# Casting x straight into its region of the activation buffer, and normalizing it there in place, in an eight-core attention and gated-MLP layer

## The reference

```python
xn = layernorm(x)                          # mean and variance over 1024 features
q, k, v = split(xn @ Wqkv + bqkv)          # 3 x 1024
q, k = q / norm(q), k / norm(k)
kv = sum over all 4096 tokens of k * v     # one row of 1024 for each batch
attn = (q * kv) @ Wout + bout
h = silu(xn @ w1.T * s1) * (xn @ w2.T * s2)      # 4096 wide
h = gelu(h @ h1.T * t1); h = gelu(h @ h2.T * t2)
out = x + attn + h @ w3.T * s3
```

## Time and profile before

| what | us |
|---|---|
| the runs shown, both | 3056.84 and 3350.54, median 3203.69 |
| the profiled execution | 3057.52 |
| its span on the slowest core (core 5) | 3055.7 |
| spans of the other cores | 3011.9 to 3048.4 |
| TensorE (PE) busy on core 5 | 2877.9 (94% of the span) |
| DVE, ACT busy | 378.7 (12%), 464.8 (15%) |
| loads of x, all through SP | 96 of 512 KB |
| loads of weights, through POOL | 416 of 512 KB landed |

### The profile page before, as it was taken

How to read it: one execution, slowest core, us unless ns; L and a number is a source line. 1 busy time by engine, 2 the same in 40 slices (tenths; PEclk the granted TensorE clock), 3 DMA queues, 4 the chain that set the end, 5 groups by cost and what they waited for, 6 DMA issues and landing times.

```text
span 3055.7 us, 30723 instructions; the slowest of 8 cores (3011.9 to 3055.7 us)
## 1 busy us (share of the span) xinstructions
PE 2877.9 (94%) x13056; PEld 1282.4 (42%) x13056; DVE 378.7 (12%) x440; ACT 464.8 (15%) x463; POOL 219.9 (7%) x420
## 2 busy tenths in 40 slices
PE   3887999899999999999987899999999999999998
PEld 0332444344444444444433344444444444444433
DVE  3255211451000000000012221100000000000011
ACT  1453211441000000000020031110000000000100
POOL 0000000110000000000000000000000000000000
PEclk8988999999999999999988999999999999999999
DMA  6555344875444444444446544444444444444453
GB/s 161 133 134 128 73 77 75 173 130 91 76 76 76 76 76 76 76 76 77 76 102 133 125 81 79 74 77 77 77 77 78 77 76 77 76 76 76 76 111 89
DMA packets 76598, 278.93 MB, mean 91 GB/s; under 512 B 8752, under 2 KB 8880, under 8 KB 76464
## 3 DMA queue, kind: packets, MB, share of 16 engines
q0 software_dynamic: 59904, 218.13, 43.1%
q1 hardware_dynamic: 16560, 58.85, 6.2%
HBM read 486.66 MB, written 8.39 MB: 162 GB/s over the span
## 4 chain that ended last, share of the span: by engine, by line
PE 83%; DMA 5%; DVE 2%; ACT 1%; issue 0%; SPq 0%; DVEq 0%; ACTq 0%
PE PD L198 23%; PE PC L198 23%; PE PB L198 19%; PE PA L198 18%; DMA xs<-x_fm 4%; DMA out_fm<-os 1%; DVE os L703 1%; DVE os L697 0%; ACT os L669 0%; DVE tmp_f L259 0%; DVE xb L210 0%; ACT Ab L628 0%; DVE Ab L500 0%; DVE Gb L261 0%; DVE tmp_f L237 0%
## 5 line engine op out<-in xcount | busy, mean ns | idle before, releaser
L198 PE MATMUL PC<-Gb,wr 128*128 128x512 bf16 x2080 | 476.3, 381 | 26.5 <-DVE Gb L261 26.5
L198 PE MATMUL PD<-Gb,wr 128*128 128x512 bf16 x2080 | 477.3, 382 | 0.0
L198 PE MATMUL PB<-Gb,wr 128*128 128x512 bf16 x1728 | 392.8, 381 | 4.2 <-DVE rstd_b L242 4.2
L198 PE MATMUL PD<-Ab,wr 128*128 128x512 bf16 x1536 | 357.7, 387 | 40.4 <-ACT os L669 40.4
L198 PE MATMUL PC<-Ab,wr 128*128 128x512 bf16 x1536 | 348.9, 380 | 2.1 <-ACT os L669 2.1
L198 PE MATMUL PA<-Gb,wr 128*128 128x512 bf16 x1536 | 347.2, 379 | 0.0
L198 PEld LDWEIGHTS PC<-Gb,wr 128*128 128x128 bf16 x2080 | 203.4, 98 | 277.9 <-issue 36.0
L198 PEld LDWEIGHTS PD<-Gb,wr 128*128 128x128 bf16 x2080 | 205.1, 99 | 250.0 <-issue 8.5
L198 PEld LDWEIGHTS PB<-Gb,wr 128*128 128x128 bf16 x1728 | 169.4, 98 | 210.5 <-issue 8.1
L191 POOL DMA_DIRECT2D wr<-h_t x256 | 135.1, 528 | 1616.6 <-PE PB L198 798.4
L198 PEld LDWEIGHTS PD<-Ab,wr 128*128 128x128 bf16 x1536 | 152.4, 100 | 231.0 <-issue 57.4
(11 more groups left out here) (87 smaller groups left out, 1002.8 us busy)
## 6 DMA issues: line engine op xcount, KB each, us to landing
wr<-h_t POOLq DMA_DIRECT2D x256, 512.0 KB, 5.2
xs<-x_fm SPq DMA_DIRECT2D x96, 512.0 KB, 5.0
wr<-w_t POOLq DMA_DIRECT2D x96, 512.0 KB, 5.7
wr<-wqkv_t POOLq DMA_DIRECT2D x56, 512.0 KB, 5.8
out_fm<-os SPq DMA_DIRECT2D x16, 512.0 KB, 3.3
wr<-wout_t POOLq DMA_DIRECT2D x8, 512.0 KB, 5.8
cst<-consts SPq DMA_DIRECT2D x1, 64.0 KB, 1.9
ones_sb<-ones_bf SPq DMA_DIRECT2D x1, 32.0 KB, 2.7
```

The costliest lines, as they stand in the source:

```text
L198: e.matmul(p[:, h * 512:(h + 1) * 512], l, r, start=a, stop=b),
```

## The change

In plan_stats a new argument via_region (true unless given) casts x into its own region of Gb, not into xb. Squares and sums read it from there. The cast waits until the region is free. In the second pass the product reads the bf16 chunk from Gb, and no second load of x is made; the subtraction overwrites the chunk in place, after the chunk's own square and sum have been read (chunk_toks). The call for group 5, made while h2's input has just been read from Gb, keeps the old way (via_region=False). Group 3 moves from region 0 to region 1, since its cast now happens while the gate still reads group 4 in region 0. So xn is now computed from x rounded to bf16. Of the 96 loads of x, 32 go: the second ones of groups 0, 1, 2 and 3.

```diff
-REGION = {0: 0, 1: 1, 2: 2, 3: 0, 4: 0, 5: 2}
+REGION = {0: 0, 1: 1, 2: 2, 3: 1, 4: 0, 5: 2}
...
-                jb, bslot, fb = xb_ring.next()
-                tb = S.op("vector", lambda e, o=bslot, i=xslot: e.tensor_copy(o[:, :], i[:, :]),
-                          waits=[tx, fb], inc="s_dv")
+                if via_region:
+                    tb = S.op("vector", lambda e, g_=g, c_=c, i=xslot: e.tensor_copy(
+                        xn_sl(g_, c_), i[:, :]),
+                        waits=[tx, war[REGION[g]]], inc="s_dv")
+                    sq_src = xn_sl(g, c)
+                else:
+                    (as before)
...
-                tq = S.op("scalar", lambda e, o=qslot, i=bslot: e.activation(o[:, :], i[:, :], AF.Square),
+                tq = S.op("scalar", lambda e, o=qslot, i=sq_src: e.activation(o[:, :], i, AF.Square),
...
-                    tok_s = mm(psS, hh, ones_sb[:, :], bslot[:, hh * 512:(hh + 1) * 512],
+                    rhs = xn_sl(g, c, hh) if via_region else bslot[:, hh * 512:(hh + 1) * 512]
+                    tok_s = mm(psS, hh, ones_sb[:, :], rhs,
...
-                xb_ring.set_free(jb, [tok_s, tq])
+                if via_region:
+                    chunk_toks[c] = [tok_s, tq]
+                else:
+                    xb_ring.set_free(jb, [tok_s, tq])
...
             def emit_xn(c):
-                jx, xslot, tx = dma_x(c, t0)
-                ta = S.op("vector", lambda e, i=xslot: e.tensor_mul(tmp_f[:, :], i[:, :], rstd_b[:, :]),
-                          waits=[tx, t5], inc="s_dv")
+                if via_region:
+                    ta = S.op("vector", lambda e, g_=g, c_=c: e.tensor_mul(
+                        tmp_f[:, :], xn_sl(g_, c_), rstd_b[:, :]),
+                        waits=[t5], inc="s_dv")
+                    tb2 = S.op("vector", lambda e, g_=g, c_=c: e.tensor_tensor(
+                        xn_sl(g_, c_), tmp_f[:, :], u_b[:, :], ALU.subtract),
+                        waits=[ta, t6, chunk_toks[c]], inc="s_dv")
+                else:
+                    (as before)
...
-                    emit_xn = plan_stats(g + 1, "PA", "PB", defer_xn=True)
+                    emit_xn = plan_stats(g + 1, "PA", "PB", defer_xn=True,
+                                         via_region=False)
```

More of the change, by code:

```diff
@@ L199, in mm, with plan_stats @@
                         waits=waits, inc=inc)
-        def plan_stats(g, psS="PA", psQ="PB", defer_xn=False):
+        def plan_stats(g, psS="PA", psQ="PB", defer_xn=False, via_region=True):
             t0 = T0MAP[g]
@@ L204, in plan_stats @@
             last_q = [None]
+            chunk_toks = {}
             for c in range(DC):
@@ L208, in plan_stats @@
                 jx, xslot, tx = dma_x(c, t0)
-                jb, bslot, fb = xb_ring.next()
-                tb = S.op("vector", lambda e, o=bslot, i=xslot: e.tensor_copy(o[:, :], i[:, :]),
-                          waits=[tx, fb], inc="s_dv")
+                if via_region:
[4 more added lines that the diff above has]
+                else:
+                    jb, bslot, fb = xb_ring.next()
+                    tb = S.op("vector", lambda e, o=bslot, i=xslot: e.tensor_copy(o[:, :], i[:, :]),
+                              waits=[tx, fb], inc="s_dv")
+                    sq_src = bslot[:, :]
                 xs_ring.set_free(jx, tb)
                 jq, qslot, fq = sq_ring.next()
-                tq = S.op("scalar", lambda e, o=qslot, i=bslot: e.activation(o[:, :], i[:, :], AF.Square),
+                tq = S.op("scalar", lambda e, o=qslot, i=sq_src: e.activation(o[:, :], i, AF.Square),
                           waits=[tb, fq], inc="s_ac")
@@ L257, in emit_xn @@
             def emit_xn(c):
-                jx, xslot, tx = dma_x(c, t0)
-                ta = S.op("vector", lambda e, i=xslot: e.tensor_mul(tmp_f[:, :], i[:, :], rstd_b[:, :]),
-                          waits=[tx, t5], inc="s_dv")
[L261 to L264, removed]
+                if via_region:
[6 more added lines that the diff above has]
+                else:
+                    jx, xslot, tx = dma_x(c, t0)
+                    ta = S.op("vector", lambda e, i=xslot: e.tensor_mul(tmp_f[:, :], i[:, :], rstd_b[:, :]),
+                              waits=[tx, t5], inc="s_dv")
+                    tb2 = S.op("vector", lambda e, g_=g, c_=c: e.tensor_tensor(
+                        xn_sl(g_, c_), tmp_f[:, :], u_b[:, :], ALU.subtract),
+                        waits=[ta, t6, war[REGION[g]]], inc="s_dv")
+                    xs_ring.set_free(jx, ta)
                 xn_toks.append(tb2)
```

## The result

| | before | changed |
|---|---|---|
| median of all runs, us | 3060.45 (10 runs) | 3025.17 (11 runs) |
| mean of the runs that the ratio compares, us | 3056.5 (7 runs) | 3020.4 (8 runs) |
| profiled execution, slowest core's span | 3055.7 (core 5) | 3013.3 (core 6) |
| mean span of the eight cores, profiled execution | 3032.3 | 2998.3 |
| loads of x | 96 | 64 |

The ratio of changed to before is 0.9882, 95% interval 0.9856 to 0.9908: a gain of 36 us, 1.2%; the interval leaves out 1, and the gain lies within the 2% that stood for "same". The forecast was 3027. Executions in which the cores of one die or of both took longer at a lower granted clock are left out of the ratio; one of them is why the two runs first shown lay 294 us apart.

A forecast was written before the change was run, and what follows sets the result against it. TensorE fills 94% of the slowest core's 3055.7 us, so only its waits can give time back. Terms 6 + 7.5 + 6.4 + 10.9 = 30.8 us, from 3057.5, gave 3027; own range 3015 to 3036, chance 0.70.

The forecast's parts named there:

- k-projection 1: First block, with xn(1): without reloads TensorE's waits for normalized chunks and the lower clock after them go; 7.5 us saved.
- segment 1: Second block: xn(3) ends earlier without reloads, so this segment runs as long as segment 2; 10.9 us saved.
- stats(2): Group 2's statistics, first block: casts start earlier after the kv sums, 12.4 us left of 18.9; 6.4 us saved.
- xn(0): Group 0's normalization at the start: product from Gb taken at 1.23 us, no wait for x before; 0 us saved.
- stats(1): Group 1's statistics, first block: casts follow their loads without waiting for xb slots; 6 us saved.
- stats(3): Group 3's statistics: loads issued only in the second block, wait on region 1 already over; 0 us saved.
- A: Rival: block 1's gain goes to the loads, x still late for stats(1) and stats(2); 18.4 us left, 3039; chance 0.12.
- B: Rival: nothing reaches the end, the slowest core waits elsewhere as long, as for os in the output stage; 3057; chance 0.06.
- C: Rival: the slowest core also loses 33 us of output-stage waits for os; 2994; chance 0.08.
- D: Rival: product from Gb costs d us over 1.23; 24d - 9.6 against 30.8, decides from d = 1.7; chance 0.04.

The follow-up runs named there:

- Four slots: Changed kernel with four f32 slots for x in the first block, not two; ratio to the kernel before 0.9861.
- group 3 alone: Changed kernel with only group 3 cast into its region; groups 0, 1 and 2 keep xb and their second loads; ratio to the kernel before 0.9987.
- the product twice: Changed kernel with each of the 32 products in place done twice; ratio to the kernel before 0.9983.
- second loads kept: Changed kernel without the xb slots, but the second pass loads x again and multiplies from the f32 slot; ratio to the kernel before 0.9974.
- x ahead of the stores: Changed kernel with both loads of x of an output pair issued ahead of the two stores in the output stage; ratio to the kernel before 0.9813.
- weights held at the start: Changed kernel with the first five weight units loaded only after the sixth cast of stats(0); ratio to the kernel before 0.9822.
- groups 0 to 2 alone: Changed kernel with group 3 as before (xb, region 0, second loads); ratio to the kernel before 0.9934.
- the run with three parts: Changed kernel with four slots for x, all of stats(3) in the first block and first weights held until the sixth cast; ratio 0.9735, median 2969.0 us.

## Why the prediction was right, step by step

**Total.** The sum was 30.8 us. In the mean of the cores segment 2, behind the last stage of the sum, starts 31.3 us earlier (614.8 to 583.5). On core 5, whose rows I read, it is 23.3 (608.5 to 585.2). Two terms were read on a core where they are smaller than the mean (k-projection 1 by 3.3 us, segment 1 by 2.4), stats(2) was put 3.4 too high, and two stages put at nothing lost time; that the sum met the mean is in part luck. So is the end: the sum put nothing on the output stage, but on the slowest core the waits for os fell from 42.5 us to 30.8 (the row from 40.4 to 28.9), which is over the 10 us that the prediction had named as a sign of being wrong. The profiled execution's slowest core gained 42 us by it, not 31, and the ratio says 36. In the mean of the cores these waits fell by 2.0 only, and the span by 34.0: there the 31.3 of the sum are nearly all of it.

| step | predicted | core 5 | mean of cores |
|---|---|---|---|
| xn(0), product at 1.23 | 0 | product 1.23 | start 0.3 earlier |
| stats(1) | 6 | 6.9 | 7.2 |
| xn(1), k-projection 1 | 7.5 | 7.6 | 10.9 |
| stats(2) | 6.4 | 3.0 | 3.1 |
| border, way to stats(3) | 0 | -3.2 | -0.5 |
| stats(3) | 0 | -1.9 | -2.3 |
| segment 1 | 10.9 | 10.4 | 12.8 |

*stats(1)*: the mechanism was right (casts at 73 to 97, forecast 74 to 95), and the stage ran nearly at ACT's pace, the fast end of 7.4. On core 5 only the first four pairs of sums from 109.2 on went at the lower clock; the granted clock of the stage is 0.85.

*k-projection 1*: right to 0.1 us. From the start of v-projection 0 to stats(2) every core needs 62.1 us; the prediction had 62.2. Before, the cores needed 69.7 to 75.7, and core 5 the least, which is why the mean gains more.

*stats(2)* is the term that was mis-sized: 12.4 us predicted, 15.4 measured. The step that failed is "the other three pairs come 5.83 us apart". On core 5 the pairs came 7.3, 7.1 and 5.2 us apart (171.34, 178.64, 185.77, 190.93). The last pair was not cast at once either, but 2.05 us apart. The pace had been taken from one pair of rows. Four slots take the term to its bound, 10.8, so the loads were late for want of slots; why two slots went slower than in the earlier trace rows is not shown (in the changed kernel the cores ask at nearly the same time, which is a guess at the cause).

*stats(3)* was put at nothing and lost 2.3 us. Counted from the first load issued behind the border to the first gate matmul, so with the first load's own time, it is 36.4 us before and 39.2 now; on core 5, where the way to stats(3) is 3.2 longer too, 36.0 and 40.7. The wait on region 1 is out (group 3 alone, 30.9). What roughly fits all nine kernels that have that stage at the border and their own weights beside it is how close together the cores start stats(3), each by its own clock: the kernel before, 11.9 us apart, needs 30.5; the product twice, 10.5 apart, 30.6; second loads kept, 8.8 apart, 30.5; group 3 alone, 8.7 apart, 30.9; x ahead of the stores, 8.2 apart, 31.7; weights held at the start, 7.2 apart, 32.3; groups 0 to 2 alone, 6.8 apart, 32.0; the changed kernel, 5.6 apart, 32.8; four slots, 5.5 apart, 32.0. That is a correlation over one profile each; no run changed the distance by itself, and the rows don't show how far the cores' clocks are apart. That cores meeting is the cause is not shown.

*Segment 1*: right. 0.5 us remained, the load of ACT's table for the segments' first logarithm, which stands in the path once xn(3) no longer hides it.

**The rivals.** A (gain handed to the loads): wrong for stats(1), half right for stats(2). B and C: the waits for os do pick the slowest core. Core 5 had 42.5 us in all and was last; in the changed kernel it has 19.2, and its own span fell by 53 us, not 31. But another core, with 30.8, took its place, so the end of the profiled execution moved by 42. C had put 33 us on these waits; the slowest core's fell by 11.7. The run with x ahead of the stores shows that a good part of these waits was the order of SP's queue. D: not met. Its formula, 24d - 9.6, gives 22.3 for the product twice (d = 1.33), and 20.7 were measured; but its stats(2) part had the wrong sign (1.4 given back, not lost), and k-projection 1 and segment 1 lost more than it says. "Each row of DVE with bf16 input at 1.23" was a little loose: L345, with bf16 in and out, takes 1.28. Nothing hangs on it.

The Trainium skill (SBUF — State Buffer, the box on DVE blocking DMA) was weighed for casts that keep POOL from writing descriptors. No run here shows a cost of the moved casts: no projection of the first block but the first output of group 0 waits for more than 0.22 us, and stats(1) is near ACT's pace. What the Trainium skill (VectorE: DVE Perf Modes, "What auto-detection actually checks") says of a product with an f32 operand agrees with the row: 1.23 us, no faster for the one bf16 operand.

## What to carry to other kernels

Buffers that two passes share can be the limit by their number: with two bf16 slots the third cast waited 32.74 us for an engine that had other work, and writing into the final place removed the slots and the second load at once. Read each term on all cores and the end on the slowest: here the core with the latest end had two of the terms well under the mean. A load queued behind a store that waits for arithmetic made the next addition late (6.05 us in the rows above); issuing it first took two lines and gave 21 us by the ratios, more than half of what the whole change gave (36). Before blaming a border between blocks, look at which engine ends last in front of it.

## What was unexpected of the hardware

- Five weight units issued beside eight loads of x cost much. In the mean of the cores the eighth cast of stats(0) comes at 40.7 us with the units issued just behind the first loads (5.47 us on core 5), at 29.1 with the units behind the sixth cast, and at 22.3 with that and four slots for x (the run with three parts).
- Behind the block border the eighth cast comes 31.5 us after the first load of x is issued, and 22.4 us after it with the weights held back on all cores.
- The block border adds 0.58 us between the last instruction of DVE and the first of TensorE; the other 4.26 us of TensorE's 4.84 are DVE's remaining work. The first output behind it takes 5.30 us, not 3.62, at a granted clock of 0.72: 1.7 us more.
